# A graph layer and mixture kernel on one core: TensorE picks rows in 32 rounds in place of 30

## The reference

```python
h = batch_norm(x @ w1.T + b1, g1, bt1)
src, dst = (edge_index[0], edge_index[1])
diff = h[src] - h[dst]
m = jax.ops.segment_max(diff, dst, num_segments=N)
m = jnp.where(jnp.isfinite(m), m, 0.0)
hg = jnp.concatenate([h, m], axis=-1)
hg = jax.nn.gelu(batch_norm(hg @ wg.T + bg, gg, btg))
out = batch_norm(hg @ w2.T + b2, g2, bt2) + res
...
x = x + gnn(_layernorm(x), edge_index, ...)
x = x + ffn(_layernorm(x)[None], ...)[0]
```

## Time and profile before

| | us |
|---|---|
| median of 3 runs | 3091.74 (3090.57 to 3094.89) |
| the profiled execution, its own time | 3090.28 |
| its span, first to last instruction | 3088.5 |
| PE busy in the span | 2730.9 (88%) |
| DVE busy | 1995.8 (65%) |
| ACT busy | 1896.6 (61%) |
| POOL busy | 1523.7 (49%), 1439.3 of it the 1444 gathers of L661 |
| mean granted TensorE clock | 0.945 of full speed |

### The profile page before, as it was taken

One profiled execution on the slowest core, in us unless ns is written; L12 is line 12 of the kernel. 1 busy time (PEld: TensorE's weight loads), 2 busy tenths in 40 slices (PEclk: granted clock), 3 DMA queues, 4 the chain that ended last, 5 costly groups with the idle time before them and its releaser, 6 DMA issues. The chain is left out here.

```text
span 3088.5 us, 38120 instructions
## 1 busy us (share of the span) xinstructions
PE 2730.9 (88%) x13907; PEld 2307.1 (75%) x13907; DVE 1995.8 (65%) x3951; ACT 1896.6 (61%) x2623; POOL 1523.7 (49%) x1538
## 2 busy tenths in 40 slices
PE   6789999998999999999999891098799999999998
PEld 6567777776777777777777691087699999999998
DVE  6776777777777677676767643398555565565644
ACT  6567676676677767776776660016456565565554
POOL 1577777777777777777777777641000000000000
PEclk9899999999999999999999995599899999999999
DMA  7567676766767666666666666521324334243231
GB/s 231 170 226 243 230 250 223 246 234 235 241 232 244 222 213 228 227 224 208 225 211 218 222 211 207 173 70 74 89 95 133 120 115 138 103 138 115 101 107 62
DMA packets 165616, 560.27 MB, mean 181 GB/s; under 512 B 31382, under 2 KB 69078, under 8 KB 158260
## 3 DMA queue, kind: packets, MB, share of 16 engines
q1 hardware_dynamic: 87780, 354.70, 31.2%
q0 software_dynamic: 77648, 203.13, 22.8%
HBM read 320.71 MB, written 237.00 MB: 181 GB/s over the span
## 5 line engine op out<-in xcount | busy, mean ns | idle before, releaser
L661 POOL DMA_INDIRECT ring<-runs,src_i x1444 | 1439.3, 997 | 516.9 <-issue 375.8
L1078 PE MATMUL ps<-oh,zhl 128*128 128x512 f32 x2940 | 1205.7, 410 | 135.6 <-DVE oh L842 123.3
L1080 PE MATMUL ps<-oh,zhl 128*128 128x512 f32 x2940 | 1177.4, 400 | 0.0
L836 DVE SCALAR_TENSOR_TENSOR ring<-ring,pen 128x256 f32<-128x256 f32 x1564 | 753.7, 482 | 574.6 <-DMA ring<-runs,src_i 547.9
L683 ACT ACTIVATE oh<-ids,nodeneg 128x512 fp32r<-128x512 f32 x840 | 601.4, 720 | 458.9 <-PE ps L1080 455.6
L1078 PEld LDWEIGHTS ps<-oh,zhl 128*128 128x128 f32 x2940 | 572.7, 195 | 293.2 <-DVE oh L842 154.5
L1080 PEld LDWEIGHTS ps<-oh,zhl 128*128 128x128 f32 x2940 | 572.3, 195 | 116.3
L688 ACT ACTIVATE oh<-oh,ones 128x512 fp32r<-128x512 f32 x840 | 574.6, 708 | 0.0
L842 DVE TENSOR_SCALAR oh<-ps,nodef 128x512 fp32r<-128x512 f32 x630 | 469.5, 745 | 18.6 <-PE ps L1080 18.0
L1641 ACT ACTIVATE av<-ps,vecs 128x896 f32<-128x896 f32 x224 | 246.3, 1100 | 329.3 <-PE ps L196 329.2
L1789 DVE TENSOR_TENSOR h2l<-av,h2h 128x896 fp32r<-128x896 f32 x112 | 122.3, 1092 | 203.6 <-ACT h2h L1643 203.6
(11 more groups left out here) (300 smaller groups left out, 3541.8 us busy)
## 6 DMA issues: line engine op xcount, KB each, us to landing
runs<-ring SPq DMA_DIRECT2D x136, 896.0 KB, 4.3
fw<-wsp SPq DMA_DIRECT2D x56, 1536.0 KB, 6.5
runs<-ring SPq DMA_DIRECT2D x102, 768.0 KB, 4.1
ring<-runs,src_i POOLq DMA_INDIRECT x1444, 3.1
ids<-srcT_d SPq DMA_DIRECT2D x30, 256.0 KB, 5.5
res_d<-x_all SPq DMA_DIRECT2D x7, 896.0 KB
y<-res_d SPq DMA_DIRECT2D x7, 896.0 KB, 7.4
part<-in_Wx SPq DMA_DIRECT2D x16, 384.0 KB, 7.1
```

Of the source, the lines that this page charges most:

```text
L661: pool.indirect_dma_start(ring[:, k, :], None, runs[0:N, :], bass.IndirectOffsetOnAxis(ap=src_i[:, STEPS * i + k:STEPS * i + k + 1], axis= ...
L836: dve.scalar_tensor_tensor(out=ring[:, k, :], in0=ring[:, before, :], scalar=pen[:, STEPS * i + k:STEPS * i + k + 1], in1=ring[:, k, :], o ...
L1078: pe.matmul(ps[:, two + k, :], z_hi(g)[:, v, cols], oh[:, v, :], start=g == 0 and v == 0, stop=False, skip_group_check=True)
L1080: r = pe.matmul(ps[:, two + k, :], z_lo(g)[:, v, cols], oh[:, v, :], start=False, stop=False, skip_group_check=True)
```

## The change

Three constants change. `PK` goes from 30 to 32, so PE picks rows in rounds 0 to 31 and the chain takes them in rounds 1 to 32. `FIRSTG` goes from 7 to 21: the looks begin, and end, two rounds later. `EARLY` goes from 19 to 21: the late product's weights are fetched and prepared two rounds later. An assertion ties the last look to round PK-1.

```diff
@@ -51,7 +51,7 @@
 NPE = 4
 PSLOT = STEPS - NPE
 PG = ROUNDS - 2
-PK = PG - 2
+PK = PG
 SLOTS = 7
 LEAD = 21
 BD = (1, 3, 5)
@@ -60,8 +60,8 @@
 GM = 4
 LASTW = E - (P - 1) * WIN
 Q = WIN // 4
-FIRSTG, BLOCKG = NG, 4
-EARLY = 2 * NE + 3
+FIRSTG, BLOCKG = 3 * NG, 4
+EARLY = 2 * NE + 5
 NZ = 6
 PIECEW = 256
 EPS = 1e-5
```

## The result

Nine runs of the changed kernel gave 3086.47 us as their median (3082.18 to 3089.93), nine of the kernel before, taken with them, 3095.16 us (3090.57 to 3099.91). The ratio is 0.9971, with a 95% interval of 0.9960 to 0.9981: 8.7 us faster, where the forecast was 9.4. The profiled execution took 3086.47 us around a span of 3084.7.

A forecast was written before the change was run, and what follows sets the result against it. The prediction took POOL's queue of 1444 gathers to bound the edge phase. Gathers removed (-10.3 us) and slower gathers beside picks (+0.9) gave -9.4, so 3091.74 became 3082.3 us, range 3078.3 to 3086.7.

The forecast's parts named there:

- The bound: Edge phase: a queue of 1444 gathers on POOL, one after another, 0.30 us between them, sets the end.
- The gathers taken away: Rounds 31 and 32: 8 fewer gathers at a pitch of 1.282 us each gain 10.3 us.
- The picks beside the gathers: Two more rounds of picks: 84 gathers beside one-hots, at 1.293 against 1.282 us, lose 0.9 us.
- the rule: GpSimd and VectorE collide in two-port modes or with two SBUF inputs; new one-hots read PSUM, so loss would be nothing.
- The late product fits: Block's end on PE: product ends at 1972.5 to 1972.9, before the next block at 1978.5, so hidden.
- The reserve of 5.6 us: PE's idle time left between the late product's end and the next block, where it was 124 us.
- The clock: After the block's end: PE's clock falls again, so no gain taken; staying up would gain 1.9 us, chance 0.06.
- The sum: Whole kernel: -10.3 + 0.9 = -9.4 us, taking the median from 3091.74 to 3082.3 us.
- The range: Whole kernel's median: 3078.3 to 3086.7 us, including the product sticking out by half a gain.
- half of 0.10: Rival at the block's end: late product sticks out a little, 3082.7 to 3087 us, chance 0.10, half still faster by 6.2.
- That the product at the lower clock ends the block: Rival at the block's end: product at half clock takes up to 59 us more, time up to 3136, chance 0.06.
- no cost: Edge phase: chain, stores and added one-hots on DVE and ACT lie in spare time, adding nothing.

The follow-up runs named there:

- no_picks: Kernel before with all 1564 rows gathered by GpSimd and PE's picks removed: 3234.28 us beside 3090.74 before, ratio 1.0470.
- tail_17: Changed kernel plus 17 dummy matmuls (3.9 us) on TensorE behind the late product: 3079.55 us beside 3089.03 before, ratio 0.9968.
- again: Changed kernel unaltered, run once more in a slow job: 3616.90 us beside 3609.53 for the kernel before, ratio 1.0025.
- pk_only: Changed kernel with FIRSTG and EARLY back at 7 and 19: 3624.48 us beside 3609.53 before, ratio 1.0034; repeat ratio 1.0032.
- gathers_alone: Kernel before with 8 gathers left out of rounds 31 and 32, no picks instead: 3602.53 us beside 3609.53, ratio 0.9976; repeat 0.9983.

## Why the prediction was right

**The bound.** Right, for executions like the one that was profiled. That POOL is the queue was read from 38 of 50 us in every stretch and from gaps of 0.30 us. One reading was too short: 210 of the gaps, 64.0 us, are put down to the chain (L836) and not to "issue"; none is longer than 0.3 us, so the reading of them as a fixed gap stands. no_picks shows it as a cause: 120 gathers more, 141.3 us more. Per gather that is 1.18 us net, and 1.293 us gross.

**The gathers taken away, -10.3 us.** Not measured alone at 3090 us; with the picks, the two traces above give 9.5 and 9.9 us from the 1265th gather on. The price of 1.282 each is 0.01 below the pitch of no_picks (1.293), which would make it 10.3 as well.

**The picks beside the gathers, +0.9 us.** The term was 84 x 0.011. no_picks gives 0.007 to 0.009 us a gather, 0.6 to 0.8 us, and the two rounds themselves ran at 1.292 as forecast. Beside the late product the pitch was 106.3 / 82 = 1.296 after and 99.1 / 77 = 1.287 in tail_17, where it had been 1.290. By the Trainium skill's GPSIMD Engine Reference (section 1, Specifications), as it was weighed in the prediction, one-hots that read PSUM should cost nothing. The traces give 0.007 to 0.009 us, two to three times the 0.003 by which two executions differ in this pitch. no_picks also leaves out more than the one-hots (ACT's copies into the ring, PE's reads, the loads of edge numbers), so the rule is neither shown nor broken by it.

**The late product fits.** Its end was forecast for 1972.5 to 1972.9 and came at 1973.7. PE's added rounds took (1871.95 - 1764.32) / 2 = 53.8 us each, 54.5 expected; the wait for `ends` was 5.3 us and not 7.2. The last picks closed at 1871.95 and not near 1868.5: the 3.0 us by which this execution was late at the 1265th gather are most of that. The reserve of 5.6 us was a little underrated: PE idles for 7.7 us before the next block, and tail_17 put 4.1 us into it for nothing.

**The clock.** Right: 0.73, then 0.50 behind the product, no gain in the next stage.

**The sum.** -9.4 against -8.7 (the interval of the ratio, 0.9960 to 0.9981, is 5.9 to 12.4 us) and -9.5 in tail_17. The range held the median of 3086.47 by 0.23 us only: of the 4.2 us above the 3082.3, 3.4 are the kernel before, whose median moved from 3091.74 to 3095.16 with the added runs, and 0.7 the change itself. That the absolute time still fell inside was in part luck; that the difference came out near the forecast was not. In the chances there is a slip of 0.01: half of 0.10 went in as 0.04.

**What it did not see.** "That the product at the lower clock ends the block" was the rival on the slower side, at 0.06. In the jobs at 3600 us the change does make the kernel slower (0.25% in `again`, 0.34 and 0.32% in the two runs of pk_only), and the late product does end the block, but by another mechanism than the one priced there: not the clock, but PE, DVE and ACT being slow to start their next instruction through most of the edge phase. In it both assumptions behind "no cost" fall, that PE keeps pace with the gathers and that the product runs beside them. Nothing in the trace before could tell that such executions exist. Why they do is open: gather issues, chain steps (0.48 us), one-hots (0.72 us) and the spacing of matmuls once they flow are the same as at 3090 us, and only the starts are late. No trace shows what holds them up.

## What to carry to other kernels

Look for the queue, not for the highest share: an engine at 49% that never waits bounded this stage, and 97 us of work for the engine at 88% went into a place where it had been idle. When a change fills such a place, work out what reserve is left (5.6 us of 124 here), and name what it relies on: the cover exists only as long as the covering engine is the slower one. Price one item of the queue by the distance of its starts, and test it with a kernel that has many more of them; 120 gathers more gave a clear answer where 8 less were at the edge of what can be measured.

## What was not expected of the hardware

- GpSimd's own speed differs between executions of one program by about 0.5%: casts of 942 against 937 ns, gather issues of 957 against 953 ns; tail_17 and no_picks have 936 and 935, and 953. On a queue of 1436 gathers this is 4 us, as much as half the effect of the change.
- Whole jobs ran 17% longer (3609.53 against 3089.03 us for the kernel before, on the same chip), nearly all in the edge phase (518 of the 529 us between the profiles of `again` and after), where the starts of instructions on PE, DVE and ACT came in steps of some 0.7 us (waits of 1.62, 2.32, 3.02 us ahead of equal matmuls), until some 16 us behind the last gather in gathers_alone. The cause is open. The sign of this change is different there.
- A gather whose issue took 2.74 us beside a DVE operation of 2.02 us with two operands in SBUF was not an accident of one run: the longest issue is 2.76 us in the profile after, 2.67 in tail_17 and 2.48 in no_picks, and in all of them each of the seven such operations of round 0 has an issue of over 1.4 us beside it.
